# Moving turned 128x1024 chunks into stacked quadrants by way of memory instead of by eight direct transfers

## What is computed

```python
def _gat_layer(x, W, adj):
    proj = x @ W
    Wh, Ws = jnp.split(proj, 2, axis=-1)
    scores = Wh @ Ws.T
    a = jax.nn.softmax(scores, axis=-1) * adj
    out = a @ Wh
    out = out + x
    return jax.nn.leaky_relu(out, NEG_SLOPE)
x0 = x
for l in range(2):
    x = _gat_layer(x, W_stack[l], adj)
return _layernorm(x0 + x)
```

## Time and profile before

| what | value |
|---|---|
| median of 3 runs | 1899.39 us (1899.38 to 1900.33) |
| time of the profiled execution | 1900.65 us |
| its span, first to last instruction | 1898.8 us |
| PE busy | 1648.5 us, 87% |
| DVE busy | 1320.6 us, 70% |
| POOL busy | 799.4 us, 42% |
| ACT busy | 654.7 us, 34% |
| share of the 16 DMA engines' span in packets of SP's queue | 56.3%, 301.10 MB |

### The profile page before, as it was taken

One profiled execution on the slowest core, in us unless ns is written; L12 is line 12 of the kernel. 1 busy time (PEld: TensorE's weight loads), 2 busy tenths in 40 slices (PEclk: granted clock), 3 DMA queues, 4 the chain that ended last, 5 costly groups with the idle time before them and its releaser, 6 DMA issues.

```text
span 1898.8 us, 23216 instructions
## 1 busy us (share of the span) xinstructions
PE 1648.5 (87%) x8104; PEld 1340.3 (71%) x8104; DVE 1320.6 (70%) x1558; ACT 654.7 (34%) x1175; POOL 799.4 (42%) x679
## 2 busy tenths in 40 slices
PE   7898889989989998988588898899889888898885
PEld 6777677777767777776477676677767767677664
DVE  4666767777677667776537777777787777777764
ACT  4333333333333333333223333333333333333331
POOL 2343334444333344443243444444444454444444
PEclk9999999999999999999889999999999999999998
DMA  4355556556655555556613565665556565655653
GB/s 161 92 163 162 153 163 168 166 161 166 167 161 163 162 167 166 164 161 176 196 54 105 164 170 167 171 173 170 164 169 173 168 170 167 170 165 163 178 169 106
DMA packets 167748, 302.57 MB, mean 159 GB/s; under 512 B 39760, under 2 KB 68432, under 8 KB 167504
## 3 DMA queue, kind: packets, MB, share of 16 engines
q1 hardware_dynamic: 167632, 301.10, 56.3%
HBM read 157.29 MB, written 9.44 MB: 88 GB/s over the span
## 4 chain that ended last, share of the span: by engine, by line
DVE 35%; SPq 34%; DMA 16%; PE 6%; issue 5%; ACT 3%; POOL 1%; POOLq 0%; ACTq 0%; DVEq 0%
SPq L223 30%; DMA load<-adj 14%; DVE ring L605 13%; DVE ring L610 8%; DVE neg_max L577 4%; DVE weight L596 2%; SPq L196 2%; PE banks L395 1%; PE banks L294 1%; SPq L200 1%; PE banks L295 1%; PE banks L296 1%; ACT ring L488 1%; DVE rows L620 1%; DVE rows L618 1%
## 5 line engine op out<-in xcount | busy, mean ns | idle before, releaser
L691 POOL TENSOR_TENSOR a_lo<-turned,a_hi 128x512 fp32r<-128x512 f32 x512 | 736.1, 1456 | 904.3 <-ACT a_hi L507 902.3
L395 PE MATMUL banks<-wh,a_hi 128*128 128x512 f32 x2048 | 792.7, 423 | 212.4 <-POOL a_lo L691 206.2
L605 DVE SCALAR_TENSOR_TENSOR ring<-ring,weight,load 128x1024 f32<-128x1024 f32 x256 | 439.8, 1718 | 362.6 <-DMA load<-adj 360.5
L395 PEld LDWEIGHTS banks<-wh,a_hi 128*128 128x128 f32 x2048 | 402.1, 196 | 387.8 <-POOL a_lo L691 237.0
L488 ACT ACTIVATE ring<-banks,neg_max 128x1024 f32<-128x1024 f32 x256 | 286.3, 1118 | 1079.2 <-DVE neg_max L577 1079.2
L397 PE MATMUL banks<-wh,a_lo 128*128 128x256 f32 x2048 | 591.3, 289 | 0.0
L294 PE MATMUL banks<-x_t,q_t 128*128 128x512 f32 x1024 | 406.4, 397 | 5.6 <-DVE x_t L541 4.0
L397 PEld LDWEIGHTS banks<-wh,a_lo 128*128 128x128 f32 x2048 | 405.1, 198 | 2.7
L296 PE MATMUL banks<-x_t,q_t 128*128 128x512 f32 x1024 | 401.9, 393 | 0.0
L295 PE MATMUL banks<-x_t,q_t 128*128 128x512 f32 x1024 | 401.5, 392 | 0.0
L577 DVE TENSOR_REDUCE neg_max<-banks 128x1 f32<-128x1024 f32 x256 | 305.0, 1191 | 39.9 <-PE banks L296 39.8
(11 more groups left out here) (65 smaller groups left out, 725.3 us busy)
## 6 DMA issues: line engine op xcount, KB each, us to landing
load<-adj SPq DMA_DIRECT2D x256, 512.0 KB, 4.0
turned<-ring SPq DMA_DIRECT2D x2048, 64.0 KB, 2.0
ring<-x SPq DMA_DIRECT2D x8, 512.0 KB, 5.1
rows<-x SPq DMA_DIRECT2D x32, 128.0 KB, 4.3
x_scratch<-rows SPq DMA_DIRECT2D x32, 128.0 KB, 3.7
ring<-x_scratch SPq DMA_DIRECT2D x8, 512.0 KB, 4.7
rows<-x_scratch SPq DMA_DIRECT2D x32, 128.0 KB, 3.8
first_rows<-x SPq DMA_DIRECT2D x32, 128.0 KB, 3.8
```

The lines of the kernel that those rows point to most:

```text
L395: nc.tensor.matmul(psum[:, bank, :], a_hi[:, s, b], wh[:, k].rearrange("p a d -> p (a d)"), start=start, stop=stop, skip_group_check=True)
L605: nc.vector.scalar_tensor_tensor(ring[:, i % RING, :], ring[:, i % RING, :], weight[:, of:of + 1], load[:, i % 2, :], ALU.mult, ALU.mult). ...
L691: nc.gpsimd.tensor_tensor(a_lo[:, j % 2].rearrange("p b (r j) -> p b r j", r=QUADS), as_f32(turned[:, unit % 2, :, b:b + SUB, :]).rearrang ...
```

## The change

`move_blocks` is split in two. `send_blocks(i)` writes the whole turned chunk to one of four 512 KB slots of a scratch tensor in memory (DRAM), as one transfer. `fetch_blocks(m)`, one step later (m = i - 1), waits for that store and brings the chunk back with two transfers, one for each quadrant of `turned`, 256 KB each: 32 partitions, each with four rows of 2 KB that lie 32 rows apart in the slot. In SP's step the order becomes: send of chunk i, load of the adjacency for chunk i + 2, fetch of chunk i - 1, refills. The ring buffer is free when the store has landed; the wait for POOL moves to the fetch.

```diff
+            def send_blocks(i):
+                sp.wait_ge(blocks_turned, i + 1)
+                if i >= BOUNCE:
+                    m = i - BOUNCE
+                    for q in range(2 * (m % 2), 2 * (m % 2) + 2):
+                        sp.wait_ge(moved[m // 2 % 2][q], 16 * (m // 4 + 1))
+                sp.dma_start(bounce[i % BOUNCE], ring[:, i % RING, :]).then_inc(bounced[i % BOUNCE], 16)
+
+            def fetch_blocks(i):
                 unit, c = i // 2, i % 2
-                u = unit % 2
-                sp.wait_ge(blocks_turned, i + 1)
+                sp.wait_ge(bounced[i % BOUNCE], 16 * (i // BOUNCE + 1))
                 if unit >= 2:
                     sp.wait_ge(lo_done, SUB * (unit - 1))
-                for q in range(2 * c, 2 * c + 2):
-                    for r in range(QUADS):
-                        sp.dma_start(as_f32(turned[QUAD * q:QUAD * (q + 1), u, r]).rearrange("p b j -> p (b j)"),
-                                     ring[QUAD * r:QUAD * (r + 1), i % RING, (q - 2 * c) * BANK:(q - 2 * c + 1) * BANK]
-                                     ).then_inc(moved[u][q], 16)
+                for q in range(2):
+                    to = 2 * c + q
+                    sp.dma_start(as_f32(turned[QUAD * to:QUAD * (to + 1), unit % 2]).rearrange("p r b j -> p r (b j)"),
+                                 bounce[i % BOUNCE].rearrange("(r j) e -> j r e", r=QUADS)[:, :, q * BANK:(q + 1) * BANK]
+                                 ).then_inc(moved[unit % 2][to], 16)
...
                 i = chunk_at(step - LAG_WEIGH)
                 if i is not None:
-                    move_blocks(i)
+                    send_blocks(i)
                     if i + 2 < LAYERS * CHUNKS:
                         load_adj(i + 2)
+                m = chunk_at(step - LAG_WEIGH - 1)
+                if m is not None:
+                    fetch_blocks(m)
```

More of the change, by code:

```diff
@@ L48, in gat_layernorm @@
     w_next_dram = nc.dram_tensor("w_next_scratch", [P, 2 * KT * 2 * D], F32).ap()
+    BOUNCE = 4
+    bounce = nc.dram_tensor("bounce_scratch", [BOUNCE, P, CHUNK], F32).ap()
     layer_in = [x, x1]
@@ L117, in gat_layernorm @@
         a_done, blocks_turned = sem("a_done"), sem("blocks_turned")
+        bounced = [sem(f"bounced{s}") for s in range(BOUNCE)]
         moved = [[sem(f"moved{u}_{q}") for q in range(QUADS)] for u in range(2)]
@@ L213, in refill_rows @@
                     load_rows(t + 2)
-            def move_blocks(i):
+            def send_blocks(i):
[6 more added lines that the diff above has]
+            def fetch_blocks(i):
                 unit, c = i // 2, i % 2
-                u = unit % 2
-                sp.wait_ge(blocks_turned, i + 1)
+                sp.wait_ge(bounced[i % BOUNCE], 16 * (i // BOUNCE + 1))
                 if unit >= 2:
                     sp.wait_ge(lo_done, SUB * (unit - 1))
-                for q in range(2 * c, 2 * c + 2):
-                    for r in range(QUADS):
-                        sp.dma_start(as_f32(turned[QUAD * q:QUAD * (q + 1), u, r]).rearrange("p b j -> p (b j)"),
-                                     ring[QUAD * r:QUAD * (r + 1), i % RING, (q - 2 * c) * BANK:(q - 2 * c + 1) * BANK]
-                                     ).then_inc(moved[u][q], 16)
+                for q in range(2):
[3 more added lines that the diff above has]
+                                 ).then_inc(moved[unit % 2][to], 16)
             load_w(0)
@@ L267, in _ @@
                         i = CHUNKS - RING + (x_slot(g) - CHUNKS) % RING
-                        for q in range(2 * (i % 2), 2 * (i % 2) + 2):
-                            sp.wait_ge(moved[i // 2 % 2][q], 64 * (i // 4 + 1))
+                        sp.wait_ge(bounced[i % BOUNCE], 16 * (i // BOUNCE + 1))
                         for p in range(2):
@@ L483, in exponentials @@
                     m = i - RING
-                    for q in range(2 * (m % 2), 2 * (m % 2) + 2):
-                        act.wait_ge(moved[m // 2 % 2][q], 64 * (m // 4 + 1))
+                    act.wait_ge(bounced[m % BOUNCE], 16 * (m // BOUNCE + 1))
                 elif i % RING >= W_SLOT:
@@ L500, in split_a @@
                     for q in range(QUADS):
-                        act.wait_ge(moved[unit % 2][q], 64 * (unit // 2 + 1))
+                        act.wait_ge(moved[unit % 2][q], 16 * (unit // 2 + 1))
                 if j % SUBS < 2:
```

## The result

The changed kernel takes **2229.68 us** (median of 4 runs, 2223.81 to 2232.84); the kernel before beside it 1899.39 us. The ratio is 1.174, 95% interval 1.171 to 1.178. It is slower, as forecast, by 330 us in place of 189, and just outside the range that ended at 2210. The profiled execution took 2232.84 us with a span of 2231.0, that is 332 us more than before, or 5.19 us for each of the 64 tiles (forecast: 2.95).

The account below looks back on a forecast made before the run. SP's issues, a load and DVE were taken to set the pace, 27.25 us a tile. With the fetch, 6.3 + 2.2 + 12.3 + 8.1 plus 1.3 for clock gives 30.2; 64 tiles add 189 us: 2088 us, range 1928 to 2210.

Parts of the forecast that it names:

- The step that decides: In SP's step at a tile's first turn, both fetches go out after T; PE's products start 8.5 us after, not 4.26.
- L: Time from T to the second fetch's landing: 6.3 us, from 1.3 start, 4.1 data and 0.9 end.
- T: End of the turn in a tile's first step (s = 0 modulo 4), from which the prediction counts its times.
- The upper bound that I gave: Fetch landing 8.2 us after T, with 6.0 us of data at the 264 GB/s of a mixed stretch.
- The clock: PE, idle about 5.3 us, then runs 3.4 us at half clock: 1.6 us, in eight tiles of ten, so 1.3.
- The other terms: Rest of a tile's chain: 2.2 us to the first product, 12.3 of products and scores, 8.1 to the next T.
- What I costed at nothing: The fetch's wait for its store, reuse of ring and slots, and the wait for POOL: no cost.
- Rival A: Adjacency load arrives early and the fetch doesn't matter, landing by T + 2.2: 125 us less, 1775; chance 0.12.
- Rival B: Fetch lands after 5.3 us and PE's clock holds: 27.7 us a tile, 29 us more, 1928; chance 0.15.
- Rival C: Slow trip through memory: landing 8.2 us after T, POOL slowed to 2.9, half clock in every tile: 2274; chance 0.10.
- Signs: Expected profile marks: DVE's, ACT's and PE's waits, PE's clock 0.93 to 0.96, SP's and DMA's chain shares, transfer counts.

Follow-up runs that it names:

- e1: Changed kernel with the fetch of chunk i - 1 issued before the wait for the turn of chunk i, not behind it; 1765.77 us, ratio 0.932.
- e5: Kernel before with a chunk's eight direct moves issued one step later, behind the next chunk's turn and the load, without memory; 2173.59 us, ratio 1.146.
- e4: Kernel before with only the adjacency load for chunk i + 2 moved ahead of the eight direct moves of chunk i; 1765.87 us, ratio 0.931.
- e3: Changed kernel with each fetch writing all 128 partitions in place of 32, same bytes, blocks in wrong places; 2158.0 us, ratio 1.138.
- e7: Changed kernel with each partition fetching slot rows 4j to 4j + 3, 4 KB apart, not 128 KB; still 32 partitions, wrong rows; 2213.89 us, ratio 1.173.
- e6: Changed kernel with 24 unread matmuls issued on PE ahead of the products that wait for the fetch, in 57 tiles; 2160.76 us, ratio 1.145.

## Why the prediction was right in kind and too small in size

- **The step that decides** (the fetch is issued behind the next turn, and only what L has over 2.2 us is paid, in full) held. e1 takes the lateness away and gains 464 us; e5 brings it back without memory and is 408 us slower than e4.
- **L, 6.3 us, was the term that was mis-sized.** It measured 8.3, 2.0 us more, or 128 us over 64 tiles, of the 142 us by which the time missed the forecast. I had priced 1.57 MB at the rates of the rows with 413 and 369 GB/s, that is 4.1 us, and the start and end of a transfer at 1.3 and 0.9. Windows of the changed kernel, of the send and the load, then of the fetch:

```profile
606.00:609.00 3.00, 1.81 (x8) 1.13 (x7) 2.97 (x3) 1.16 (x2) 0.00 (x0) 1.00 1.01 316
609.00:612.00 3.00, 0.00 (x0) 0.00 (x0) 1.56 (x2) 0.00 (x0) 0.00 (x0) 1.00 1.06 215
```

  The engines were full (shares 1.01 and 1.06) and moved 316 and then 215 GB/s. By the packets' records, as a mean of the 52 tiles, the first packet ran at T + 0.9 and the fetch's last at T + 7.4, so the start was shorter than priced and the end right; in the 6.5 us between them 1.8 MB went by. The rate, 280 GB/s, was most of the error: 1.57 MB at it take 5.6 us, 1.5 more than priced. A fetch writes 32 partitions, and my rates came from transfers over all 128; e3 with e7 shows that this is 0.9 us of it. The rest of the 1.5 is open: the send and the load, over all 128, ran at 316. The Trainium skill (SBUF — State Buffer, section on the DMA port swizzle) says that a transfer's rate goes by how many of 16 ports its partitions reach, and that 32 neighbouring partitions reach only 8; the runs agree in direction, by the 0.9 us, and I had not weighed it. The amount was about 0.25 MB more, or 0.9 us: a row refill of 128 KB and the start of the next chunk's send (issued at 608.42) run before the fetch's last packet. With 0.4 us less for the start that makes the 8.3. The amount is read from the trace, and no run takes it alone. The upper bound that I gave, 8.2, came near by luck: it had a rate of 264 GB/s, but only 1.57 MB.
- **The clock**, forecast 1.3 us a tile, cost 1.8 (4.7 and 4.8 us for the first products in the two layers, in place of 2.92). The idle piece was 7.4 us long in layer 1 and 5.9 in layer 2, not 5.3 (7.63 in the tile above), the spell at 0.51 there lasted 6.8 us (window 613.00 to 619.80) and not 3.4, and every tile of the 52 paid, not eight in ten. The Trainium skill's rule (TensorE: Matmul & The Clock Gate, HAM oscillation: every round pays) was nearer than my eight in ten, and e6 shows that it is the idle time that does it.
- **The other terms** were right to 0.2 us in layer 1: 2.02 for `a_hi`, `a_lo` and the first product (2.2), 9.3 from the end of those products to the last max (2.79 + 2.92 + 2.95 + 0.72 = 9.4), 8.1 from there to the next T (8.1). With +2.0 for L and +0.5 for the clock, 30.2 becomes the 32.45 that was measured. In layer 2 one more term was off, which I had taken to be the same in both layers: the stretch up to the last max took 10.3 us. There PE also stops for `a_lo` inside later products, 63 times in the 600 us from 1300, against 18 in those from 200. The other kernels have it too (e4: 24.64 us from T to T in layer 1, 25.7 in layer 2).
- **What I costed at nothing** was nearly nothing: over the whole span SP waited 9.1 us for a store to land before a fetch, and 1.4 us for POOL.

```profile
SPq L235 <- DMA bounce_scratch<-ring: 9.1, 19, 1.3
SPq L232 <- POOL a_lo L704: 1.4, 1, 1.4
```

- **Rival A** (the early load makes it faster) named the right price and the right condition: with the fetch in time, 1766 was measured in e1 and in e4 where 1775 had been worked out. It only wasn't met. **Rival B** had L and the clock wrong. **Rival C** was right on L (8.2) but would have POOL slowed, which it wasn't: from the start of `a_hi` to the first product it stayed at 2.03 us.
- Signs: DVE's wait 62.1 us (under 60 expected, so just missed), PE's 477.5 (over 300), SP's chain share 5% (under 15%), DMA's up from 16% to 18%, 435 MB: as said. ACT's wait for the fetch was 381.9 us, not 250, and wasn't ACT's longest. The clock was 0.89, under the 0.93 to 0.96 expected.

## What to carry to other kernels

When issues are moved to a later step of a queue that waits in order, find out which wait then stands ahead of them, and count from there to the consumer: here fewer and larger transfers gained nothing, because their result closed a ring of waits. Here the only thing worth having, a load issued 5 us sooner, cost a swap of two lines (e4), and the same bytes through memory were free (e1) as soon as they were issued ahead of the wait instead of behind it. Price a burst by the rate of the same shape (partitions written, pieces) in a full queue, and where a ring stretches and TensorE stands idle in it, expect its clock to fall too (here from 0.97 to 0.90 in the mean).

## What was unexpected of the hardware

- A fetch of 2 x 256 KB into 32 partitions each landed 0.9 us later than the same pieces into 128 partitions (e7 against e3). With 4 rows 128 KB apart L was 0.3 us more than with 4 rows next to each other (the changed kernel against e7), which the times don't confirm.
- 435 MB through one queue cost no more than 301 MB (e1 against e4: 1765.77 and 1765.87 us), though in the 600 us from 200 the engines were taken for 83% of the time at 264 GB/s, against 67% at 183.
- A fetch that was issued ahead of a row refill and of the next chunk's store ended after 1.8 MB had gone by, about 0.25 MB more than stood ahead of it and in it (mean of 52 tiles).
